# Expert gates spread over the partitions by DMA instead of by a matmul a chunk

## The reference

```
up_s = einsum('th,seh->tse', xt, shared_up)            # 2 shared experts of 64 rows
shared = einsum('tse,she->th', gelu(up_s), shared_down)
probs = softmax(xt @ router_w.T)                       # 16 routed experts
topk_p, topk_i = top_k(probs, 4)
gate = zeros_like(probs).at[arange(T)[:, None], topk_i].add(topk_p)
up_r = einsum('th,reh->tre', xt, routed_up)            # 16 experts of 64 rows
act = gelu(up_r) * gate[:, :, None]
routed = einsum('tre,rhe->th', act, routed_down)
x = x + shared + routed
```

## Time and profile before

| | us |
|---|---|
| median of 3 runs | 244.8 |
| lowest, highest | 243.49, 247.01 |
| the profiled execution | 242.17 |
| its span, first to last instruction | 240.1 |

### The profile page before, as it was taken

How to read it: one execution, slowest core, us unless ns; L and a number is a source line. 1 busy time by engine, 2 the same in 40 slices (tenths; PEclk the granted TensorE clock), 3 DMA queues, 4 the chain that set the end, 5 groups by cost and what they waited for, 6 DMA issues and landing times.

```text
span 240.1 us, 4896 instructions
## 1 busy us (share of the span) xinstructions
PE 191.1 (80%) x1610; PEld 139.0 (58%) x1610; DVE 171.0 (71%) x456; ACT 146.4 (61%) x277; POOL 95.0 (40%) x177
## 2 busy tenths in 40 slices
PE   0640778849869969969969779977987998999992
PEld 0220556726646747647647557545766876788771
DVE  4666698844856977968949969614878759878782
ACT  8364137636537547747647556786693896776760
POOL 8449605953533745646537445672202100000000
PEclk9999999998988999999999999999997999999999
DMA  3397345363363364463562540010000001010011
GB/s 91 74 316 129 76 63 59 46 80 61 48 78 60 47 78 65 57 83 48 79 69 51 64 67 26 4 27 5 22 4 1 0 3 45 0 44 0 0 44 45
DMA packets 23735, 12.97 MB, mean 54 GB/s; under 512 B 4696, under 2 KB 23400, under 8 KB 23712
## 3 DMA queue, kind: packets, MB, share of 16 engines
q1 hardware_dynamic: 23616, 12.65, 31.0%
q0 software_dynamic: 96, 0.03, 0.1%
HBM read 3.86 MB, written 1.05 MB: 20 GB/s over the span
## 4 chain that ended last, share of the span: by engine, by line
PE 40%; DMA 19%; SPq 12%; DVE 10%; issue 9%; ACT 6%; POOL 2%; POOLq 0%; DVEq 0%; ACTq 0%
DMA sb_qk_op<-sb_qk 14%; SPq L325 8%; PE psum L932 4%; DMA sb_den<-sb_o_raw 3%; PE psum L914 3%; DVE sb_mx L746 3%; PE psum L853 3%; PE psum L850 3%; PE psum L893 3%; PE psum L851 3%; PE psum L837 3%; PE psum L835 3%; PE psum L836 3%; DMA sb_x<-in_x 2%; PE psum L842 2%
## 5 line engine op out<-in xcount | busy, mean ns | idle before, releaser
L746 DVE TENSOR_REDUCE sb_mx<-psum 128x2 f32<-128x512 f32 (+1 forms) x96 | 63.4, 682 | 28.7 <-PE psum L893 17.9
L557 ACT ACTIVATE sb_probs<-psum 128x512 f32<-128x512 f32 x96 | 55.6, 604 | 36.1 <-PE psum L914 35.4
L408 POOL TENSOR_SCALAR_AFFINE_SELECT sb_probs<-sb_probs 128x256 f32<-128x256 f32 (+1 forms) x96 | 45.8, 489 | 53.5 <-ACT sb_probs L557 53.0
L890 PE MATMUL psum<-sb_fut,sb_id_b 128*128 128x256 bf16 x64 | 18.4, 287 | 25.3 <-DMA sb_qk_op<-sb_qk 15.7
L501 ACT ACTIVATE sb_probs<-psum 128x512 f32<-128x512 f32 x36 | 21.4, 598 | 13.6 <-PE psum L837 13.3
L637 DVE TENSOR_TENSOR sb_probs<-sb_probs,psum 128x512 f32<-128x512 f32 x32 | 21.9, 684 | 10.3 <-ACT sb_probs L501 10.0
L893 PE MATMUL psum<-sb_qk_op 96*128 96x256 bf16 x128 | 26.0, 286 | 0.0
L914 PE MATMUL psum<-sb_qk_op 128*128 128x256 bf16 x128 | 25.1, 279 | 0.9 <-ACT sb_probs L557 0.7
L644 DVE TENSOR_TENSOR sb_hid_l<-sb_probs,sb_hid_h 128x512 fp32r<-128x512 f32 x36 | 24.7, 685 | 0.3
L890 PEld LDWEIGHTS psum<-sb_fut,sb_id_b 128*128 128x128 bf16 x64 | 6.8, 107 | 29.8 <-DMA sb_qk_op<-sb_qk 17.3
L507 ACT CAST sb_hid_h<-sb_probs 128x512 fp32r<-128x512 f32 x36 | 22.2, 616 | 2.9 <-DVE sb_probs L637 2.9
(11 more groups left out here) (113 smaller groups left out, 401.5 us busy)
## 6 DMA issues: line engine op xcount, KB each, us to landing
sb_qk_op<-sb_qk SPq DMA_DIRECT2D x96, 64.0 KB
sb_ctx<-in_ctx_t SPq DMA_DIRECT2D x8, 128.0 KB, 4.9
sb_num<-sb_o_raw SPq DMA_DIRECT2D x8, 128.0 KB, 2.5
out<-sb_o_raw SPq DMA_DIRECT2D x4, 256.0 KB, 2.3
sb_x<-in_x SPq DMA_DIRECT2D x3, 256.0 KB, 5.7
sb_probs<-in_rup_t SPq DMA_DIRECT2D x1, 512.0 KB, 5.8
sb_probs<-in_rdown SPq DMA_DIRECT2D x1, 512.0 KB, 6.9
sb_x<-in_x SPq DMA_DIRECT2D x2, 128.0 KB, 2.4
```

Of the source, the lines that this page charges most:

```text
L408: nc.gpsimd.affine_select(out=v, in_=v, compare_op=ALU.is_ge, fill=0.0, base=0, pattern=[[0, v.shape[1]], [1, P]], channel_multiplier=-1). ...
L557: nc.scalar.activation(probs[g][:, u * BANK:(u + 1) * BANK], psum[:, BANK_S + n % SB, :], ACT.Exp, scale=float(DH) ** -0.5).then_inc(s_exp, 1)
L746: nc.vector.tensor_reduce(dst, src, AX, ALU.max).then_inc(m_max, 1)
L890: mm(v[:, :, P:2 * P], id_b[:, :], fut[:, :].unsqueeze(1).to_broadcast([P, 2, P]), start=True, stop=False, skip_group_check=True)
```

## The change

`spr`, `g_parts` and the fourth matmul of `up` go. `gate` is padded with zeros and transposed in fp32 as it is, so that `gate_t` holds 16 experts on 16 partitions. For each block n, SP writes `gate_t`'s 512 columns to a DRAM tensor `gate_d`, waits, and reads them back with 8 DMAs, one for each routed chunk. Each takes the two rows (2 KB each) of the chunk's experts and writes them 64 times, alternately, to the 128 partitions of `gates[n % 2]`, 256 KB a DMA and 2 MB a block. These two buffers lie over the attention operands `qk_op`. For that, the hidden rows of two experts are interleaved in the weights (by strided copies of `up` in ACT and POOL and by two strided loads for `down`). DVE multiplies by `gates` from SBUF. The freed PSUM banks 3 and 4 make 5 banks for `up`. For k = 0, ACT writes the gelu where DVE's copy went. The `low` of chunks 2, 5 and 8 moves from DVE to POOL, with a semaphore of its own. The loops over n = 2, 3 are written out.

```
@@ sizes
-        UP_BANKS, NF = 3, 4
+        UP_BANKS, NF = 5, 4
+        POOL_LOW = (2, 5, 8)
+        gates = [o[:, :, :, :].rearrange("p h n s -> p (h n s)").bitcast(F32).rearrange("p (c q) -> p c q", q=BANK)
+                 for o in qk_op]
@@ SP
+            def load_gates(n):
+                cols = slice(n * BANK, (n + 1) * BANK)
+                sp.wait_ge(gt_read, BANK // S * (n + 1) + 1)
+                sp.dma_start(gate_d[:, cols], gate_t[:, cols]).then_inc(gate_out, 16)
+                if n < 2:
+                    sp.wait_ge(s_ps, UNITS * (NB - 1 + n))
+                else:
+                    sp.wait_ge(hid_done, (NCH - 1) * (n - 1))
+                sp.wait_ge(gate_out, 16 * (n + 1))
+                for k in range(1, NCH):
+                    rows = gate_d[2 * (k - 1):2 * k, cols]
+                    sp.dma_start(gates[n % 2][:, k - 1, :], rows.partition_broadcast(P // 2))\
+                        .then_inc(gates_in[n % 2], 16)
...
+                if isinstance(turn.at, int) and turn.at in (NB + 1, NB + 2):
+                    load_gates(turn.at - NB - 1)
...
+            for n in range(NCT):
+                if n + 2 < NCT:
+                    load_gates(n + 2)
                 sp.wait_ge(y_done, n + 2)
@@ POOL
+            def low(n, k):
+                pool.wait_ge(hid_hi, n * NCH + k + 1)
+                pool.wait_ge(d_ps, count(n * NCH + k - NF + 1))
+                nc.gpsimd.tensor_tensor(hid_l[buf[k]][:, :], hid[buf[k]], hid_h[buf[k]][:, :].bitcast(F32),
+                                        ALU.subtract).then_inc(hid_low, 1)
...
-                        nc.gpsimd.tensor_copy(g_parts[:, :, 0, :], gate[:, :, :]).then_inc(g_step, 1)
...
+                    routed = [u[:, P:NCH * P].rearrange("e (k j h) -> e k h j", h=2, k=NCH - 1) for u in (up_l, up_h)]
...
-            nc.gpsimd.memset(spr[:, :].bitcast(F32), 0.0).then_inc(pads_set, 1)
+            nc.gpsimd.memset(gate[:, :, :, :], 0.0).then_inc(pads_set, 1)
@@ ACT, gelu
+                nc.scalar.activation((hid if k == 0 else gel)[buf[k]], psum[:, at % UP_BANKS, :], ACT.Gelu)\
+                    .then_inc(u_gelu, 1)
@@ DVE, gated
+                dve.wait_ge(u_gelu, n * NCH + k + 1)
+                after_low(dve, *before(n, k))
+                dve.wait_ge(gates_in[n % 2], 16 * (NCH - 1) * (n // 2 + 1))
+                nc.vector.tensor_tensor(hid[buf[k]], gel[buf[k]], gates[n % 2][:, k - 1, :], ALU.mult).then_inc(hid_done, 1)
@@ DVE, chunk
+                if k > 0:
+                    gated(n, k)
+                if k > 0 and k - 1 not in POOL_LOW:
                     low(n, k - 1)
@@ PE, up
-                if k > 0:
-                    pe.wait_ge(hid_done, count(at - 1) if isinstance(at, int) else at - 1)
-                    mm(psum[:, 3 + k % 2, :], spr[:, P * (k - 1):P * k], gate_t[:, cols], start=True, stop=True).then_inc(gate_ps, 1)
@@ PE, step 11
-                        pe.wait_ge(g_last, count(c + 1))
+                        pe.wait_ge(r_step, count(RSTEPS * (c + 1)))
```

More of the change, by code:

```diff
@@ L168, in xattn_moe_kernel @@
         gsel = sb("gsel", [P, QB, NR], F32)
[L169 to L174 removed]
+        gate = sb("gate", [P, QB, P // NR, NR], F32)
+        gate_t = sb("gate_t", [NR, T], F32)
+        gate_d = nc.dram_tensor("gates_by_expert", (NR, T), F32, kind="Internal").ap()
+        UP_BANKS, NF = 5, 4
+        POOL_LOW = (2, 5, 8)
         DOWN_LAG = 3
@@ L210, in xattn_moe_kernel @@
         r_ps, r_exp, r_step = sem("r_ps"), sem("r_exp"), sem("r_step")
-        g_step, g_last = sem("g_step"), sem("g_last")
         gt_ps, gt_read = sem("gt_ps"), sem("gt_read")
-        u_ps, gate_ps, u_gelu, hid_done = sem("u_ps"), sem("gate_ps"), sem("u_gelu"), sem("hid_done")
+        u_ps, gates_in, u_gelu, hid_done = sem("u_ps"), [sem(f"gates_in{s}") for s in range(2)], sem("u_gelu"), sem("hid_done")
+        hid_low = sem("hid_low")
         hid_hi, hid_lo, d_ps, d_read, y_ps, y_done = (sem("hid_hi"), sem("hid_lo"), sem("d_ps"), sem("d_read"),
@@ L234, in early_chunk, with after_low, before @@
             return None if m is None else divmod(m, NCH)
+        def after_low(eng, n, k):
+            if n < 0:
+                return
+            if k in POOL_LOW:
+                eng.wait_ge(hid_low, len(POOL_LOW) * n + POOL_LOW.index(k) + 1)
+            else:
+                eng.wait_ge(hid_lo, (NCH - len(POOL_LOW)) * n + len([j for j in range(k) if j not in POOL_LOW]) + 1)
+        def before(n, k):
+            return (n, k - NF) if NF <= k < NCH - 1 else (n - 1, k + NF if k < NF else k)
         def last_scores(turn):
@@ L456, in turn_of @@
                                                 xh[:, bass.ds(c * S, S)].bitcast(F32), ALU.subtract).then_inc(xl_done, 1)
+                    at = early_chunk(turn, t)
+                    if at is not None and at[1] in POOL_LOW:
+                        low(*at)
                 if not isinstance(turn.at, int):
@@ L481, in _ @@
             attention(turn_of)
+            for n in range(1, NCT):
+                for k in POOL_LOW:
+                    if n * NCH + k >= len(early):
+                        low(n, k)
         @block.scalar
@@ L499, in gelu @@
                 act.wait_ge(u_ps, at + 1)
-                act.wait_ge(hid_done, count(at - NF + 1))
-                nc.scalar.activation(gel[buf[k]], psum[:, k % UP_BANKS, :], ACT.Gelu).then_inc(u_gelu, 1)
+                if k == 0:
+                    after_low(act, *before(n, k))
+                else:
+                    act.wait_ge(hid_done, count((NCH - 1) * n + k - NF))
+                nc.scalar.activation((hid if k == 0 else gel)[buf[k]], psum[:, at % UP_BANKS, :], ACT.Gelu)\
+                    .then_inc(u_gelu, 1)
             def high(n, k):
                 at = n * NCH + k
-                act.wait_ge(hid_done, at + 1)
+                if k == 0:
+                    act.wait_ge(u_gelu, at + 1)
+                else:
+                    act.wait_ge(hid_done, (NCH - 1) * n + k)
                 act.wait_ge(d_ps, count(at - NF + 1))
@@ L592, in turn_of @@
                         act.wait_ge(gt_ps, count(c + 1))
-                        nc.scalar.copy(gate_t[:, bass.ds(c * S, S)], psum[:, BANK_A, 0:S])\
+                        nc.scalar.copy(gate_t[:, bass.ds(c * S, S)], psum[0:NR, BANK_A, 0:S])\
                             .then_inc(gt_read, 1)
@@ L618, in _ @@
                 chunk(1, k, False)
-            with act.Fori(2, NCT) as n:
+            for n in range(2, NCT):
                 for k in range(NCH):
@@ L717, in choose @@
                     after(10)
-                    nc.vector.tensor_tensor(gate[:, :, :], gsel[:, :, :], rexs[:, :].unsqueeze(2).to_broadcast([P, QB, NR]),
+                    dve.wait_ge(gt_ps, count(c))
+                    nc.vector.tensor_tensor(gate[:, :, 0, :], gsel[:, :, :], rexs[:, :].unsqueeze(2).to_broadcast([P, QB, NR]),
                                             ALU.mult).then_inc(r_step, 1)
@@ L812, in _ @@
                 chunk(1, k, False)
-            with dve.Fori(2, NCT) as n:
+            for n in range(2, NCT):
                 for k in range(NCH):
                     chunk(n, k, False)
-            low(NCT - 1, NCH - 1)
             finish(NCT - 1)
@@ L1064, in _ @@
             pe.wait_ge(gt_read, NB + 1)
-            with pe.Fori(2, NCT) as n:
+            for n in range(2, NCT):
                 for k in range(NCH):
```

61 lines of the change are left out of this document (23 added, 38 removed).

## The result

| | before | changed |
|---|---|---|
| median of the runs on one chip, us | 244.15 (4 runs) | 256.02 (4 runs) |
| lowest, highest | 240.06, 247.01 | 253.68, 262.21 |
| profiled execution, its span | 242.17, 240.1 | 253.68, 251.7 |

The ratio is 1.056, with a 95% interval of 1.030 to 1.081: **slower**, where I forecast no change.

What follows compares the result with a forecast made beforehand. PE was taken as the bound from 202 us, DVE's `att` chain as its wait in turns 9 to 11. 242.2 + 0.8 - 2.0 - 2.1 = 238.9 us, as a median 241.5, no measurable change; range 236 to 272.

Steps and rivals of the forecast that it cites:

- X of 7.6 us: Gate loads: time from a block's first read issued to its last landing, taken as 7.6 us.
- +0.8 us at the output projection: Turns 9 and 10: block 0's gates delay DVE's first product, so `att` comes 0.8 us later for PE.
- Rival 1: Gate loads: reading one row 64 times is slow; 15% for a mild form (243 to 257 us), 27% for a strong one.
- The rule on large distances: Gate loads: copies fall to 103 GB/s with rows a large power of two apart; the sum would be about 283 us.
- Issue of eight reads, 0.5 each: SP's queue: after a block's write, SP issues its 8 gate reads at about 0.5 us each.
- After turn 11, -2.1: Chunks from 202 us: 3.7 us of `up` matmuls saved, less 1.0 and 0.6 of new costs, together -2.1 us.
- the +0.6 of the forecast: Kernel's end: the last chunk's `low` runs on POOL instead of DVE, making the closing chain 0.6 us longer.
- The stall at a block's end: PE waits about 0.5 us for ACT's bank read after blocks 1 and 2, and once more in turn 11.
- Turn 11, -2.0: Turn 11: nine matmuls (2.1 us) and a 0.41 us wait go, one block end costs 0.5; together -2.0 us.
- The 0.41 of the gates' wait: Turn 11: PE's 0.41 us wait for POOL's split before the last gates are transposed would go.
- The wait for `att` at 3 us or more: Sign before batch 7's output projection: PE waits 3 us or more for DVE's `att`, then runs at low clock.
- Rival 3: POOL becomes late with 3 `low`s a block, costing PE 11 x 0.5 = 5 us, result 246 to 247; 6%.

Runs made afterwards that it cites:

- e6: Changed kernel with the two rows of a read adjacent in DRAM, 2 KB apart instead of 8 KB; median 244.9 us.
- e1: Changed kernel with each read taking 128 different rows of the input x, 2 KB apart (values wrong); 242.9 us, ratio 1.012 to the kernel before.
- e7: Changed kernel with eight gate copies in DRAM, a read's 16 rows one 32 KB piece, each read 8 times; two runs, 270.4 and 276.6 us.
- e2: Changed kernel with one 256 KB read a block instead of eight, all products using its gates (values wrong); 239.3 us, ratio 0.984 to the kernel before.
- e11: Changed kernel with a read's two rows adjacent and a semaphore for each read; median 239.2 us, ratio 0.994 to the kernel before.
- e16: As e11, but the `low` of chunks 2 and 5 goes back to DVE; median 236.6 us, ratio 0.990 to the kernel before.
- e14: Changed kernel with the rows of the DRAM tensor 24 KB apart instead of 8 KB; median 252.0 us.

## Why the prediction was wrong, step by step

- **X of 7.6 us, "the lower end with little added": this step failed.** It was 15.3 to 16.1. The sum had +0.8 us at the output projection for block 0's reads, where PE's first stretch grew by 11.2, and nothing for blocks 1 and 3, where 10.3 and 11.1 us seemed free; DVE waited 11.06, 3.30 and 5.91 us in blocks 0, 1 and 3. I knew X as the weakest choice and bounded it from 7.3 to 93, then took the end that the loads of different rows gave. Even the fast layouts need 9.0 to 10.3 from first read to product, so 7.6 was short in the best layout by some 2 us.
- **Rival 1 had the right price and the wrong mechanism.** With the measured X its formula gives 7.7 + 5.8 + 4.9 = 18.4 us; PE's stretches lost 90.1 - 71.9 = 18.2 to the reads. Block by block it fits less well (3.3 us of waiting in block 1, not 5.8). But reading a row 64 times is not slow in itself (e6). The loads that landed late were `bo` and `exno`, and I took them as evidence on repetition. What makes those two late was not tried. The range of 236 to 272 holds the measured 256.0 thanks to this rival, not to the forecast.
- **The rule on large distances that stood beside it was nearer the cause.** Two rows 8 KB apart are slow, 10 KB are not. The Trainium skill, "DMA: Bandwidth & Descriptors" (section Latency and other measured facts), tells of a like fall for row distances of 512 KB and more, and of padding as the repair; with its 103 GB/s the time would have been the 283 of the prediction, an estimate. The trace shows 160 GB/s, already at 8 KB, and at 24 KB, which is no power of two.
- **Issue of eight reads, 0.5 each.** A single issue takes 0.43 us in e1 and 0.61 in e6 and in the changed kernel (medians). The eight together take 3.7 to 3.9, 5.1 to 6.0 and 6.8 to 7.2 us; in the slow kernel single issues reach 1.8. That the busy DMA engines held SP up is argued only: e7's eight issues take 4.9, with an X of 16.8.
- **After turn 11, -2.1: right.** 33.3 in e2 against 35.2. Chunks follow each other in 1.40 us; the last `up` to the last `down` takes 246.44 - 242.51 = 3.9 against 3.3, the +0.6 of the forecast. The stall at a block's end is there, but it is 0.29 us and not 0.5. The changed kernel has it after block 1, e2 after blocks 1 and 2; after block 2 the late gates hide it in the changed kernel:

```profile
214.35 0.40 PE L882 MATMUL psum<-sb_xh,sb_up_l 128*128 128x512 f32 x1
215.04 0.50 PE L890 MATMUL psum<-sb_hid_h,sb_dn_h 128*128 128x512 f32 x1 [0.29 <-ACT sb_o_raw L562]
```

- **Turn 11, -2.0: too much.** -0.8 in e2, and +0.9 in e11, where PE runs more of it at the lower clock (0.83 over 180 to 200 us; e2 1.00, before 0.91). The 0.41 of the gates' wait did not go; it became 0.95, for the reason in the last section.
- **The wait for `att` at 3 us or more: right in number, by luck.** It is 3.27 us in e2 without any slow read, against 2.17. Of these 1.1 us, 1.0 is a cost that I did not have. The `low` of chunk (0,5), which I took off DVE's list for a gain of 0.6, runs on POOL just when DVE makes batch 6's gate, right ahead of `att`; DVE's `gsel` then takes 1.18 us against 0.17 before. These are `gsel` before, and `gsel` and POOL's `low` in the changed kernel:

```profile
180.62 0.17 DVE L716 TENSOR_TENSOR sb_gsel<-sb_ex,sb_chosen 128x32 f32<-128x32 f32 x1
```

```profile
186.19 1.18 DVE L760 TENSOR_TENSOR sb_gsel<-sb_ex,sb_chosen 128x32 f32<-128x32 f32 x1
```

```profile
186.05 1.26 POOL L450 TENSOR_TENSOR sb_hid_l<-sb_probs,sb_hid_h 128x512 fp32r<-128x512 f32 x1 [5.96 <-ACT sb_hid_h L557]
```

  In e16, with that `low` back on DVE, `gsel` takes 0.17 again. The stretch to the projection is 1.0 longer in e2 than before, where the same working without a wait for reads gives 0.9 less. That matmuls taken out ahead of `att` only lengthen the wait is not shown: little of the 1.1 us is left for them.
- **Rival 3, POOL late:** 1.34 us each, and no `down` waits for POOL but the last. It did not happen. POOL and DVE do hinder each other, but it was DVE that became late.

In all, the parts other than the reads were worth -1.8 us in PE's three stretches, about half of the 4.1 that I had. By its times e2 gains more, 1.0 to 2.2% or 2.5 to 5.2 us; what lies between is ahead of the first mark, where the profiles scatter by more than that. The reads took 18 us.

## What to carry to other kernels

Before a matmul is replaced by a broadcast through DRAM, look at the DRAM address of the rows that one DMA alternates between: here the natural layout [experts, tokens] put them 8 KB apart and nearly halved the rate, and laying the block's rows side by side cost nothing. Give each transfer its own semaphore where the consumer takes them in order; that alone took the ratio from 1.056 to 1.014. And where a price is bounded only by far ends, the forecast is a bet on that price: say at which value the verdict turns (12.4 us for 2% here) and put the range over it. Work moved to another engine is not free either when the two engines hinder each other: here it made operations late that stood on the critical path.

## What the runs showed of the hardware

- Two rows read 64-fold by one DMA: 284 GB/s at 2 KB apart (e6), 164 GB/s at 8 KB (changed kernel) and 160 GB/s at 24 KB (e14); at 16 KB, X is the same as at 8. 128 rows are hardly slowed by 8 KB (10.0 us against 9.0), and 16 rows on half of the engines not at all. The cause inside the memory was not measured.
- A leading repeat of 8 left the DMA engines at a busy share of 0.57 and 159 GB/s.
- DVE and POOL hinder each other. DVE's gate (32 columns) takes 0.19 us, but in turn 11 of the changed kernel it took as long as POOL's `low` beside it, as `gsel` did in turn 10:

```profile
206.71 1.25 DVE L764 TENSOR_TENSOR sb_gate<-sb_gsel,sb_rexs 128x32 f32<-128x32 f32 x1
```

```profile
206.64 1.27 POOL L450 TENSOR_TENSOR sb_hid_l<-sb_probs,sb_hid_h 128x512 fp32r<-128x512 f32 x1 [4.49 <-ACT sb_hid_h L557]
```

The Trainium skill, "SBUF — State Buffer" (section SBUF: two separate sides), says that a VectorE operation with two SBUF inputs and a GpSimd operation that reads SBUF exclude each other for a whole instruction. These two rows agree, and in e16, which has no `low` on POOL there, PE's wait for the gate is gone. The change takes the product's gates from PSUM to SBUF and puts a `low` on POOL, and I had priced neither with the other in mind. The products met it too: single ones take 1.19 to 1.21 us in e2 and in the changed kernel, against 0.68.
